# A graph network kernel: the row of node weights moved to ScalarE's queue, and its weighted sums spread one per unit

## The reference

```python
h = relu(layernorm(x))
h = sigmoid(h @ wenc.T + benc)                 # 500 features
agg = segment_sum((h @ conv)[src] * edge_weight[:, None], dst)
x = x + (agg + h @ lin.T) @ wdec.T + bdec
h = relu(layernorm(x))
deg = number of edges leaving each node, + 1   # self loops
norm = deg[row] ** -0.5 * deg[col] ** -0.5     # edges and self loops
x = x + segment_sum(norm[:, None] * (h @ W.T + b)[col], row)
```

## Time and profile before

| | us |
|---|---|
| median of 3 runs | 475.68 (475.54 to 477.18) |
| the profiled execution | 475.57 |
| its span | 473.8 |
| TensorE busy | 462.5 |
| VectorE busy | 316.0 |
| ScalarE busy | 203.1 |

### The profile page before, as it was taken

One profiled execution on the slowest core, in us unless ns is written; L12 is line 12 of the kernel. 1 busy time (PEld: TensorE's weight loads), 2 busy tenths in 40 slices (PEclk: granted clock), 3 DMA queues, 4 the chain that ended last, 5 costly groups with the idle time before them and its releaser, 6 DMA issues.

```text
span 473.8 us, 9213 instructions
## 1 busy us (share of the span) xinstructions
PE 462.5 (98%) x3472; PEld 401.6 (85%) x3472; DVE 316.0 (67%) x606; ACT 203.1 (43%) x408; POOL 35.2 (7%) x36
## 2 busy tenths in 40 slices
PE   6999999999999999999899999999999999999997
PEld 5899999978888888889788887888889988888885
DVE  5989886777857852694558777838652656667642
ACT  6985674655542231232425544547342622222220
POOL 3300000000000000000000000365500000000000
PEclk9999999999999999999999999999999999999999
DMA  8820133392113670439430004252969316546542
GB/s 309 253 81 23 66 74 136 93 342 68 66 67 79 128 244 2 112 109 352 181 122 1 0 2 159 108 211 80 376 243 373 145 24 243 199 177 223 188 185 86
DMA packets 37440, 70.26 MB, mean 148 GB/s; under 512 B 16817, under 2 KB 25275, under 8 KB 35731
## 3 DMA queue, kind: packets, MB, share of 16 engines
q1 hardware_dynamic: 37074, 69.24, 42.2%
q0 software_dynamic: 320, 0.39, 0.4%
HBM read 44.33 MB, written 22.01 MB: 140 GB/s over the span
## 4 chain that ended last, share of the span: by engine, by line
PE 91%; DVE 6%; ACT 1%; DMA 1%; issue 0%; POOL 0%; SPq 0%; DVEq 0%; ACTq 0%; POOLq 0%
PE bank L1312 23%; PE bank L1313 22%; PE bank L1314 22%; PE bank L1328 18%; PE bank L1424 2%; DVE stats L969 2%; PE bank L1426 1%; PE bank L1428 1%; PE bank L1444 1%; DVE we L560 1%; DMA h<-x 1%; DVE wd_lo L560 1%; DVE h0T L1065 0%; ACT wd_hi L813 0%; DVE wc L560 0%
## 5 line engine op out<-in xcount | busy, mean ns | idle before, releaser
L1328 PE MATMUL bank<-a,h_hi 128*128 128x256 f16 (+3 forms) x400 | 85.5, 270 | 0.0
L1328 PE MATMUL bank<-a,h_lo 128*128 128x256 f16 (+3 forms) x400 | 85.5, 270 | 0.0
L1312 PE MATMUL bank<-right,left 128*128 128x512 f32 x140 | 54.5, 390 | 0.0
L1314 PE MATMUL bank<-right,left 128*128 128x512 f32 x140 | 54.5, 389 | 0.0
L1313 PE MATMUL bank<-right,left 128*128 128x512 f32 x140 | 54.5, 389 | 0.0
L1298 DVE SCALAR_TENSOR_TENSOR x<-bank,dis_u,x 128x512 f32<-128x512 f32 (+1 forms) x35 | 26.3, 751 | 37.8 <-PE bank L1314 37.8
L933 ACT CAST left<-zs 128x512 fp32r<-128x512 f32 x35 | 21.7, 625 | 63.5 <-PE bank L1314 63.5
L1312 PE MATMUL bank<-h0T,we 128*128 128x256 f32 (+3 forms) x160 | 46.3, 289 | 1.4 <-DVE h0T L1065 0.8
L1313 PE MATMUL bank<-h0T,we 128*128 128x256 f32 (+3 forms) x160 | 44.8, 280 | 0.0
L1314 PE MATMUL bank<-h0T,we 128*128 128x256 f32 (+3 forms) x160 | 44.7, 280 | 0.0
L1312 PE MATMUL bank<-unit,g 128*128 128x500 f32 (+3 forms) x120 | 42.3, 353 | 0.4 <-DVE unit L1171 0.4
(11 more groups left out here) (150 smaller groups left out, 1082.6 us busy)
## 6 DMA issues: line engine op xcount, KB each, us to landing
right_scratch<-right SPq DMA_DIRECT2D x5, 2048.0 KB, 8.2
right<-right_scratch SPq DMA_DIRECT2D x5, 2048.0 KB, 7.6
whole<-w SPq DMA_DIRECT2D x7, 1024.0 KB, 7.5
adj_scratch<-stage SPq DMA_DIRECT2D x50, 125.0 KB, 1.9
raw<-adj_scratch SPq DMA_DIRECT2D x2, 2500.0 KB, 9.1
h<-x SPq DMA_DIRECT2D x9, 512.0 KB, 6.1
x<-x SPq DMA_DIRECT2D x9, 512.0 KB, 6.9
out<-x SPq DMA_DIRECT2D x18, 256.0 KB
```

The costliest lines, as they stand in the source:

```text
L1312: pe.matmul(o, lhs[0], rhs[0], start=first, stop=False, skip_group_check=True)
L1314: return pe.matmul(o, lhs[1], rhs[0], start=False, stop=last, skip_group_check=True)
L1328: ins = pe.matmul(o, h1[i][0:n, k, 128 * f:128 * (f + 1)], moving, start=(k == 0 and part == 0 and i == 0), stop=(k == T - 1 and part == p ...
```

## The change

The step `row` moves from SyncE's program to ScalarE's: the two DMAs and the wait between them are the same, but ScalarE issues them, and SyncE passes on to the two transposes. And `rowsum` k now stands behind `sk` (1, k) for k = 0 to 9. VectorE's order becomes: units (1, 0) to (1, 2), degrees, sum 0, unit (1, 3), sum 1, unit (1, 4), and so on to unit (1, 9), then sums 7, 8 and 9.

```diff
     steps += [("general",)]
-    sums = list(range(T))
     for n in range(NS):
...
             if (n, k) == (1, 0):
                 steps += [("degrees",), ("row",), ("flip", T - 2), ("flip", T - 1)]
-            if n == 1 and k > 2:
-
-                steps += [("rowsum", sums.pop(0)) for _ in range(1 if k in (4, 6) else 2) if sums]
+            if n == 1:
+
+                steps += [("rowsum", k)]
...
                     load_raw(n, raw_in[n])
-                elif s[0] == "row":
-
-                    sp.wait_ge(dis_ready, 1)
-                    with nc.allow_non_contiguous_dma("single words"):
-                        sp.dma_start(row.rearrange("t p -> p t"), dis[:]).then_inc(row_out, 16)
-                    sp.wait_ge(row_out, 16)
-                    sp.dma_start(dis_row[:], row.rearrange("t p -> (t p)").unsqueeze(0).broadcast_to([P, NODESP])).then_inc(row_in, 16)
                 elif s[0] == "flip":
...
                     act.wait_ge(deg_sums, 1)
                     nc.scalar.activation(dsq[:], deg[:], ACT.Sqrt).then_inc(dsq_ready, 1)
+                elif s[0] == "row":
+
+                    act.wait_ge(dis_ready, 1)
+                    with nc.allow_non_contiguous_dma("single words"):
+                        act.dma_start(row.rearrange("t p -> p t"), dis[:]).then_inc(row_out, 16)
+                    act.wait_ge(row_out, 16)
+                    act.dma_start(dis_row[:], row.rearrange("t p -> (t p)").unsqueeze(0).broadcast_to([P, NODESP])).then_inc(row_in, 16)
```

## The result

The changed kernel takes 482.52 us (median of five executions, 481.49 to 482.87), the kernel before 475.68; the ratio of executions compared side by side is 1.0114, 95% interval 1.0097 to 1.0132. The executions of the kernel before lie in two groups, around 475.6 and 477.1 us, so its median stands for the lower one, and the experiments are read by their ratios to executions beside them and by their traces. The time lies in the range that was forecast, and 1.8 us over the predicted 480.7. The profiled execution takes 482.52 us as well, with a span of 480.7 against 473.8.

A forecast was written before the change was run, and what follows sets the result against it. TensorE, 98% busy, was taken as the bound; 475.57 us for the profiled execution plus a 5.0 us stall made 480.6, and 0.1 for the runs' median gave 480.7, range 479.6 to 483.4; all other terms counted as nothing.

The forecast's parts named there:

- What bounds the kernel: Whole kernel: TensorE is busy 98% of the span and full around the edit, so the change can win nothing there.
- The sums moved forward: Second third: unit (1, 3) is cut late behind the first sum on VectorE, so TensorE starts it 5.0 us later.
- What is late next: Units behind (1, 3): VectorE's 1.97 us a pair outpaces TensorE's 2.72 a unit, so one stall, not seven.
- TensorE's clock: Products behind the stall: a clock fall would cost about 1.9 us; taken as nothing.
- The rival with the fallen clock: At the unit (1, 3) stall: TensorE's clock falls, 1.0 to 1.9 us more, 481.7 to 482.6; chance 0.29.
- the plain stall: At unit (1, 3): TensorE waits 5.0 us once and the clock stays up, 480.7 us; chance 0.53.
- The trip on ScalarE's queue: The row's write and fetch from ScalarE: still 10.7 and 4.4 us, 15.1 in all, as from SyncE.
- The second rival: At the row's write: it lands faster from ScalarE's queue, no stall, 475.7 us; chance 0.09, including stalls under 2.4 us.
- ScalarE alone would just keep pace: At unit (1, 3): ScalarE's high cut, delayed to about 191.2, would not by itself hold up TensorE past 192.41.
- Past SyncE's queue: Transposes 8 and 9 go out behind the raw-count load and may delay it 0 to 2.8 us; taken as nothing.

The follow-up runs named there:

- the sums alone: The kernel before with one sum behind each unit of the second third, SyncE still issuing the row's DMAs: 483.89 us, ratio 1.015.
- the first sum two units later: The changed kernel with every sum moved two units later, the row still on ScalarE's queue: 479.31 us, ratio 1.0038.
- The run with the filled stall: The changed kernel with 32 matmuls that nothing reads ahead of unit (1, 3)'s products: 482.68 us, ratio 1.0123.
- the forty-byte runs: The changed kernel with the weights written to DRAM as 128 runs of 40 bytes, so the sums use other weights: 476.51 us, ratio 0.9987.
- the queue alone: The kernel before with only the row's two DMAs moved to ScalarE, the sums in their old places: 478.12 us, ratio 1.0022.
- the corrected ring: The changed kernel, ring-buffer wait now counting each third's last unit, unit (1, 3) cut before the degrees, sum 0 behind unit (1, 4): 474.89 us, ratio 0.9953.

## Why the prediction was right, and where it was off

*What bounds the kernel.* Right: TensorE was full, so the change could only lose, and every microsecond of the loss is one in which TensorE waited or ran slow.

*The sums moved forward.* Right in place and cause: one wait at unit (1, 3), behind the first sum, shown by the sums alone (1.015) and undone by the first sum two units later (no wait behind it) or by a row that comes early (0.9987). The size was 4.5 us and not 5.0, since the row was there at 194.77 and not 195.21: the load landed 0.5 us later, the write took 10.1 and the fetch 4.0 us in place of 10.7 and 4.4. From the sum's start to the end of the cut it was 196.16 + 0.68 - 194.77 = 2.07 us, forecast 2.06; the handover 0.14, forecast 0.1.

*What is late next.* Right: the stall does not repeat, the pair takes 1.97 us, and nothing behind it is later than the shift.

*TensorE's clock.* This is the term that was mis-sized: I took nothing, and it measured 2.2 us, a little over the upper bound of 1.9 that I had drawn from the opening. The rule of the Trainium skill that the prediction cites had spoken for it, and the last 3.4 us of the trace of before had made me leave it out of the sum. That row was cut off too early. It ends with the span at 473.8; TensorE's last product ended at 470.26, and the same view goes on behind the span:

```profile
474.00:475.00 1.00, 0.00 (x0) 0.00 (x0) 0.00 (x0) 0.00 (x0) 0.00 (x0) 0.50 0.00 0
```

So the trace of before had an idle of TensorE in which the clock fell, 3.7 us after its last product, and what the prediction took as keeping the clock up was only the first part of that idle. The rival with the fallen clock, which had a chance of 0.29 and was forecast at 481.7 to 482.6, is what happened. The run with the filled stall shows in its trace that the slow products are the clock's.

*The number.* That the time lies so near the plain stall is in part luck: the stall was 0.5 us shorter than forecast, which took back a part of the clock's 2.2. The ratio, 1.0114, is nearer still to the forecast's 1.0106, but that does not speak for a stall without the clock: it is taken against all executions of the kernel before, those of 477.1 us too, and against them 482.52 is 5.4 us more.

*The trip on ScalarE's queue.* Right that the trip does not shorten: over the traces the write takes 10.1 to 12.2 us from ScalarE and 10.7 to 12.3 from SyncE. By the Trainium skill's rule on issuing engines ("DMA: Bandwidth & Descriptors", section "Issuing engines are not separate DMA queues") another issuer does not shorten it, and the traces agree. The second rival falls: what a shorter trip would give is real (the forty-byte runs), but another queue does not bring it. Wrong was a smaller step, that ScalarE alone would just keep pace: TensorE waits 0.8 to 2.0 us for it by itself (the queue alone, and the first sum two units later). The forecast's own figures, 191.2 + 0.63 + 0.67 = 192.5, were already past 192.41, and left out the handovers from ScalarE to VectorE and on to TensorE, some 0.1 us each; in the queue alone the load landed 0.6 us later besides, and in the other run the write took 11.9 us in place of 10.7. It did not count in the changed kernel, where VectorE is later still.

*Past SyncE's queue.* Nearly right: about 0.5 us of delay to the load, where I took 0 of 0 to 2.8.

What stays open is why the same write of 1280 single words takes 10.1 us in one trace and 12.3 in another. The traces go by sets: 10.7 and 10.1 in the kernels before and after, 10.7 to 11.1 in the first set of experiments (chip 2), 11.9 and 12.2 in the second (chip 0), 12.1 in the third (chip 6), 12.3 and 11.2 in the fourth (chip 0). That looks like the chip or the time more than like the edit or the queue, but no kernel was traced in two sets.

## What to carry to other kernels

When a step that waits for a DMA is moved forward on an in-order engine, count what stands behind it and when the bottleneck wants that: here a wait moved ahead of one 0.68 us cut cost 6.9 us between the traces, ten times the cut. With the first sum two units later nothing waited behind it, but one unit still waited 2.0 us for ScalarE; with one more unit cut ahead of the trip, which needed the corrected ring, a single wait of 0.8 us was left. A stall of the matrix engine can cost its length and then a stretch at half clock: the stalls of 4.3, 5.4 and 6.0 us here all did, for about 2 us more, and one of 2.0 us did not. A forecast that ends with such a stall should carry that second term. When a row is to show that something did not happen, look at what follows right behind its end. And ask of a slow little DMA what shape it has before asking which queue it is on: the same 5 KB took 10 to 12 us as single words and 1.4 us as runs of forty bytes.

## What was not expected of the hardware

- The clock fell 2.3 us into the changed kernel's wait, and 3.7 us behind the last product of the kernel before, and a shorter wait can bring it down too: behind the wait of 1.7 us ahead of `p` it stayed at 1.00 in the traces of the kernels before and after, and fell in those of the queue alone and of the forty-byte runs. In the trace of the queue alone the stretch behind that wait reads:

```profile
235.00:240.00 5.00, 5.00 (x17) 3.92 (x16) 0.88 (x2) 0.00 (x0) 0.00 (x0) 0.66 1.04 402
```

From the first `p` product to the end of the span it is 476.4 - 234.61 = 241.8 us there, and 473.8 - 233.53 = 240.3 before, 1.5 us more. That is about the distance between the two groups of the kernel before; that its slower executions are those in which the clock fell there is likely, but no trace of one was kept.

- A VectorE operation of 1280 columns takes 2.58 us when it reads one float32 operand with a step of ten words, and 1.46 us for 1250 columns when it reads it in a row. The Trainium skill ("SBUF — State Buffer", section "Door 1: The DMA port swizzle") describes a cost for each access that leaves a line of 16 bytes; the two rows agree.
- The landing of a write of single words lies far behind the work that the DMA engines show for it, from either queue: they are 0.02 busy in the last 8.7 us before, and 0.00 in the last 6.6 us of the changed kernel's write.
